# Second attention of a four-layer kernel: a shift chain of four operations with ScalarE's copy and its rows in two lots, and selections dealt out anew over the steps

## The reference

```python
def _L1_attn_ref(x, w_attn, w_proj):
    H, HEAD_D = 16, 8                      # D = 128
    qkv = x @ w_attn
    q = qkv[..., :D].reshape(Bv, Tv, H, HEAD_D).transpose(0, 2, 1, 3)
    k = qkv[..., D:D + HEAD_D]
    v = qkv[..., D + HEAD_D:]
    att = jnp.einsum('bhqd,bkd->bhqk', q, k) * scale
    att = jnp.where(causal[None, None, :, :], att, -jnp.inf)
    att = jax.nn.softmax(att, axis=-1)
    y = jnp.einsum('bhqk,bkd->bhqd', att, v)
    y = y.transpose(0, 2, 1, 3).reshape(Bv, Tv, D)
    return y @ w_proj
```

## Time and profile before

| | us |
|---|---|
| median of 3 runs | 826.43 (826.15 to 827.19) |
| the profiled execution | 826.32 |
| its span, first to last instruction | 824.6 |
| PE busy | 658.2 |
| DVE busy | 567.6 |
| ACT busy | 348.2 |
| POOL busy | 348.9 |

### The profile page before, as it was taken

How to read it: one execution, slowest core, us unless ns; L and a number is a source line. 1 busy time by engine, 2 the same in 40 slices (tenths; PEclk the granted TensorE clock), 3 DMA queues, 4 the chain that set the end, 5 groups by cost and what they waited for, 6 DMA issues and landing times. The chain is left out here.

```text
span 824.6 us, 14720 instructions
## 1 busy us (share of the span) xinstructions
PE 658.2 (80%) x4409; PEld 408.9 (50%) x4409; DVE 567.6 (69%) x1843; ACT 348.2 (42%) x748; POOL 348.9 (42%) x510
## 2 busy tenths in 40 slices
PE   1589898987008999999965779899898989898684
PEld 1346565655005788777842234445454535353353
DVE  8378888886862322444366978798979898884373
ACT  0422223311703222323321047677676767676751
POOL 0165555661027777677511014343434344333320
PEclk9999999999558999999965669999999999999995
DMA  9300000000411222222234304030303031200020
GB/s 295 97 1 1 0 1 0 0 2 1 144 38 49 43 42 36 39 42 40 24 76 62 45 11 59 4 60 10 53 14 51 21 43 26 37 2 4 1 77 27
DMA packets 40353, 32.47 MB, mean 39 GB/s; under 512 B 3608, under 2 KB 36936, under 8 KB 40280
## 3 DMA queue, kind: packets, MB, share of 16 engines
q1 hardware_dynamic: 30448, 23.51, 13.2%
q0 software_dynamic: 7840, 6.86, 5.7%
q10 hardware_dynamic: 1992, 1.21, 0.9%
HBM read 13.60 MB, written 8.13 MB: 26 GB/s over the span
## 5 line engine op out<-in xcount | busy, mean ns | idle before, releaser
L1613 ACT ACTIVATE pexp<-wide 128x512 f32<-128x512 f32 (+2 forms) x384 | 181.5, 535 | 108.8 <-PE wide L1802 107.3
L1544 POOL TENSOR_SCALAR_AFFINE_SELECT pexp<-pexp 128x256 f32<-128x256 f32 x256 | 105.0, 414 | 202.5 <-ACT pexp L1613 200.3
L1419 DVE CUSTOM_DVE_ANT_0 masked<-bank,mask_qk 128x384 f32<-128x384 f32 (+3 forms) x356 | 154.4, 480 | 22.0 <-PE bank L1753 21.1
L1802 PE MATMUL wide<-qT,kTe 128*128 128x256 bf16 (+3 forms) x512 | 121.8, 305 | 10.2 <-ACT pexp L1613 5.2
L1753 PE MATMUL bank<-kTm,qT 128*128 128x384 bf16 (+3 forms) x356 | 90.9, 323 | 16.4 <-DVE mx L1419 10.2
L1070 ACT ACTIVATE hT<-wide,b1T 128x512 f32<-128x512 f32 x64 | 44.0, 687 | 137.2 <-PE wide L1090 137.2
L1419 DVE CUSTOM_DVE_ANT_0 masked<-wide,mask_qk 128x256 f32<-128x256 f32 (+3 forms) x156 | 74.2, 498 | 18.6 <-PE wide L1753 18.6
L938 POOL DMA_INDIRECT x_row<-xln_dram,row_u x64 | 63.4, 991 | 52.8 <-DVE slot_tok L815 33.6
L1815 PE MATMUL bank<-pexp,vx 128*32 128x512 f32 (+3 forms) x1024 | 83.5, 444 | 0.0
L945 POOL DMA_INDIRECT x_dram<-yg,row_u x40 | 63.8, 1595 | 31.3 <-DVE yg L994 21.6
L561 POOL TENSOR_TENSOR kv<-kx,qv 128x1024 f32<-128x1024 f32 x32 | 62.3, 1949 | 24.1 <-PE wide L636 24.1
(11 more groups left out here) (232 smaller groups left out, 1086.7 us busy)
## 6 DMA issues: line engine op xcount, KB each, us to landing
qT<-qp SPq DMA_DIRECT2D x135, 64.0 KB
x_sb<-in_L_attn_x SPq DMA_DIRECT2D x8, 256.0 KB, 6.9
w_sb<-in_L_ffn_w SPq DMA_DIRECT2D x1, 2048.0 KB, 12.8
xln_dram<-rx SPq DMA_DIRECT2D x8, 256.0 KB, 2.3
out_x<-x_sb SPq DMA_DIRECT2D x8, 256.0 KB, 2.3
x_dram<-x_sb SPq DMA_DIRECT2D x5, 256.0 KB, 3.5
x_sb<-x_dram SPq DMA_DIRECT2D x5, 256.0 KB, 2.9
x_row<-xln_dram,row_u POOLq DMA_INDIRECT x64, 2.5
```

Source lines behind the costliest of these rows:

```text
L1419: ins = nc.vector.tensor_tensor_reduce(out=masked[:, n % 4, at], in0=bank_of(n)[:, at], in1=mask_qk[:, T - w:T], scale=1.0, scalar=LEAST, ...
L1544: nc.gpsimd.affine_select(out=pexp[:, at, :, 0:P], in_=pexp[:, at, :, 0:P], pattern=[[0, 2], [1, P]], compare_op=ALU.is_ge, fill=0.0, base ...
L1613: nc.scalar.activation(pexp[:, exp_slot(b, 2 * step + h // 2), h % 2:h % 2 + nh, 0:w], psE[m % 3][:, 0:nh * w].rearrange("p (h t) -> p h t ...
L1802: ins = nc.tensor.matmul(psE[m % 3][:, hh * w:(hh + 1) * w], kTe[:, par, j * P:(j + 1) * P], qT[:, b % QB, 4 * qd + h + hh, j * P:T], star ...
```

## The change

Four things, all in the second attention.

1. `split` has four operations instead of five: the last subtraction writes the third part as bf16 at once, in place of a subtraction and a copy. It serves the shift (VectorE), q (VectorE; the operation at 5 C goes) and k (GpSimd).
2. The copy to `mT` moves from VectorE to ScalarE (`act_shift_T`), at the head of its step 13, behind the exponentials of step 13 and ahead of those of step 14. TensorE's transposes move from 12 D to 13 A, behind the first scores of step 14.
3. The one DMA of the shift's rows becomes six: for quad 0 one for each part (4 heads each), then for the other three quads one for each part (12 heads each). The scores of step 0 wait for the first three, those of step 4 for the last three.
4. `IN_STEP` changes from (4,3,2,2,1,2,2,2,5,4,3,3,2,4,2,3) to (4,4,4,3,1,2,2,2,4,4,3,3,1,2,2,3). `AHEAD`, the selections of steps 12 to 15, falls from 11 to 8, and steps 0 to 3 take 15 instead of 11. The order within each turn and the banks follow from the same rule as before.

```diff
+        SPLITS = 2 * PARTS - 2
...
-        IN_STEP = (4, 3, 2, 2, 1, 2, 2, 2, 5, 4, 3, 3, 2, 4, 2, 3)
+        IN_STEP = (4, 4, 4, 3, 1, 2, 2, 2, 4, 4, 3, 3, 1, 2, 2, 3)
...
             for n in ops:
                 if n:
                     engine.wait_ge(sig.sem, sig.at(b, n))
+                if n == SPLITS - 1:
+                    on.tensor_tensor(parts[-1], rest, parts[-2], ALU.subtract).then_inc(sig.sem, 1)
...
-        def dve_shift_T(dve, b):
-            dve.wait_ge(q_mTp.sem, q_mTp.at(b, 1))
-            dve.wait_ge(q_mrow.sem, q_mrow.at(b, 0))
-            nc.vector.tensor_copy(mT[:, :], psA[:, :].bitcast(BF16)[0:PARTS * HEADS, 0:T]).then_inc(q_mT.sem, 1)
...
+        def act_shift_T(act, b):
+            act.wait_ge(q_mTp.sem, q_mTp.at(b, 1))
+            for rows in q_mrow:
+                act.wait_ge(rows.sem, rows.at(b, 0))
+            nc.scalar.activation(mT[:, :], psA[:, :].bitcast(BF16)[0:PARTS * HEADS, 0:T], ACT.Copy).then_inc(q_mT.sem, 1)
...
             for s in range(STEPS):
+                if middle and s == SHIFT_STEP + 1:
+                    act_shift_T(act, b + 1)
...
             sp.wait_ge(q_mT.sem, q_mT.at(b, 1))
-            sp.dma_start(qT[QR:QR + PARTS, b % QB, :, :], mT[:, :]).then_inc(q_mrow.sem, 16)
+            for rows, lo, hi in ((q_mrow[0], 0, 4), (q_mrow[1], 4, HEADS)):
+                for n in range(PARTS):
+                    sp.dma_start(qT[QR + n:QR + n + 1, b % QB, lo:hi, :],
+                                 mT[n * HEADS + lo:n * HEADS + hi, :]).then_inc(rows.sem, 16)
...
             if step == 0:
-                pe.wait_ge(q_mrow.sem, q_mrow.at(b, 1))
+                pe.wait_ge(q_mrow[0].sem, q_mrow[0].at(b, PARTS))
                 pe.wait_ge(q_kTe.sem, q_kTe.at(b, 1))
+            if step == NT:
+                pe.wait_ge(q_mrow[1].sem, q_mrow[1].at(b, PARTS))
...
+                    if middle and (s, place) == (SHIFT_STEP + 1, "A"):
+                        pe_shift(pe, b + 1, front)
                     if place == "D":
                         if s % 2:
                             pe_values(pe, b, s - 1)
                             pe_values(pe, b, s)
-                        if middle and s == SHIFT_STEP:
-                            pe_shift(pe, b + 1, front)
```

More of the change, by code:

```diff
@@ L1190, in build @@
         Q = lambda name, per=1, step=1: signal("mqa_" + name, per, step)
+        SPLITS = 2 * PARTS - 2
         q_init = Q("buffers_set")
         q_xln, q_xTp, q_xT, q_qp = Q("xln", NT), Q("xT_psum"), Q("xT"), Q("q_psum")
-        q_kvp, q_kv, q_kpart, q_qpart = Q("kv_psum"), Q("kv"), Q("k_parts", 5), Q("q_parts", 5)
+        q_kvp, q_kv, q_kpart, q_qpart = Q("kv_psum"), Q("kv"), Q("k_parts", SPLITS), Q("q_parts", SPLITS)
         q_v, q_kx = Q("v"), Q("k_slots", PARTS)
@@ L1209, in build @@
         PER_QUAD = NM // NQ
-        q_smp, q_mx, q_mpart = Q("max_scores_psum", NM), Q("max", NM), Q("max_parts", 5)
-        q_mTp, q_mT, q_mrow = Q("max_T_psum"), Q("max_T"), Q("shift_rows", 1, 16)
+        q_smp, q_mx, q_mpart = Q("max_scores_psum", NM), Q("max", NM), Q("max_parts", SPLITS)
+        q_mTp, q_mT = Q("max_T_psum"), Q("max_T")
+        q_mrow = [Q(f"shift_rows_{lot}", PARTS, 16) for lot in ("first_quad", "other_quads")]
         NX = NQ * NT * 2
@@ L1255, in build @@
         XLN_STEPS, XT_STEP, Q_STEP, KV_STEP, K_SPLIT_STEP, SLOT_STEP, KT_STEP = (0, 1), 2, 3, 5, 6, 7, 8
-        Q_SPLIT_STEPS = (4, 5)
+        Q_SPLIT = {(4, "A"): 1, (4, "C"): 2, (5, "A"): 3}
         RESIDUAL_STEP = 6
@@ L1362, in fill_k_slots, with split @@
             return ops(kx3[:, :, :, n, :], kp[:, n].unsqueeze(2).broadcast_to([P, NT, PARTS, L]))
-        def split(engine, on, sig, b, whole, rest, parts, ops=range(2 * PARTS - 1)):
+        def split(engine, on, sig, b, whole, rest, parts, ops=range(SPLITS)):
             for n in ops:
-                part = parts[n // 2]
                 if n:
                     engine.wait_ge(sig.sem, sig.at(b, n))
-                if n % 2 == 0:
-                    on.tensor_copy(part, whole if n == 0 else rest).then_inc(sig.sem, 1)
+                if n == SPLITS - 1:
+                    on.tensor_tensor(parts[-1], rest, parts[-2], ALU.subtract).then_inc(sig.sem, 1)
+                elif n % 2 == 0:
+                    on.tensor_copy(parts[n // 2], whole if n == 0 else rest).then_inc(sig.sem, 1)
                 else:
-                    on.tensor_tensor(rest, whole if n == 1 else rest, part, ALU.subtract).then_inc(sig.sem, 1)
+                    on.tensor_tensor(rest, whole if n == 1 else rest, parts[n // 2], ALU.subtract).then_inc(sig.sem, 1)
         def dve_q_parts(dve, b, ops):
@@ L1388, in pool_k_slots @@
         def pool_k_slots(pool, b):
-            pool.wait_ge(q_kpart.sem, q_kpart.at(b, 5))
+            pool.wait_ge(q_kpart.sem, q_kpart.at(b, SPLITS))
             pool.wait_ge(q_kTp.sem, q_kTp.at(b, 0))
@@ L1462, in dve_turn @@
                         dve_shift(dve, b + 1)
-                    if middle and s == SHIFT_STEP + 1 and place == "A":
-                        dve_shift_T(dve, b + 1)
                     if middle and s < SHIFT_STEP:
@@ L1472, in dve_turn @@
                         dve_stats(dve, b - 1)
-                    if front and s in Q_SPLIT_STEPS and place in "AC":
-                        dve_q_parts(dve, b + 2, (2 * Q_SPLIT_STEPS.index(s) + "AC".index(place) + 1,))
+                    if front and (s, place) in Q_SPLIT:
+                        dve_q_parts(dve, b + 2, (Q_SPLIT[s, place],))
         def dve_ln3_shift(dve, lo, hi):
@@ L1495, in mqa_dve @@
             dve_moe_stats(dve, 4)
-            dve_q_parts(dve, 0, range(1, 5))
+            dve_q_parts(dve, 0, range(1, SPLITS))
             nc.vector.memset(mask_qk[:, 0:T - P], 0.0)
@@ L1511, in mqa_dve @@
             dve_max(dve, 0, range(PER_QUAD, 2 * PER_QUAD), bank_at_start)
-            dve_q_parts(dve, 1, range(1, 5))
+            dve_q_parts(dve, 1, range(1, SPLITS))
             dve_max(dve, 0, range(2 * PER_QUAD, NM), bank_at_start)
             dve_shift(dve, 0)
-            dve_shift_T(dve, 0)
             dve_max(dve, 1, range(AHEAD), bank_in_turn)
@@ L1625, in act_yT, with act_turn @@
             nc.scalar.activation(y2T[:, :], psT[:, :], ACT.Copy).then_inc(q_yT.sem, 1)
-        def act_turn(act, b, tail=True, front=True):
+        def act_turn(act, b, tail=True, middle=True, front=True):
             for s in range(STEPS):
+                if middle and s == SHIFT_STEP + 1:
+                    act_shift_T(act, b + 1)
                 if s % NT == 0 and (s or b):
@@ L1676, in mqa_act @@
             act.wait_ge(s_shift.sem, s_shift.total(4))
+            act_shift_T(act, 0)
             act_exp(act, 0, 0)
             for b in range(B):
-                act_turn(act, b, tail=b > 0, front=b + 2 < B)
+                act_turn(act, b, tail=b > 0, middle=b + 1 < B, front=b + 2 < B)
             act_quad(act, B - 1, NQ - 1)
@@ L1690, in q_rows @@
             for n in range(PARTS):
-                queue.wait_ge(q_qpart.sem, q_qpart.at(b, 2 * n + 1))
+                queue.wait_ge(q_qpart.sem, q_qpart.at(b, min(2 * n + 1, SPLITS)))
                 for j in range(PARTS):
@@ L1779, in pe_shift @@
         def pe_shift(pe, b, front):
-            pe.wait_ge(q_mpart.sem, q_mpart.at(b, 5))
+            pe.wait_ge(q_mpart.sem, q_mpart.at(b, SPLITS))
             if front:
```

## The result

The changed kernel takes 823.06 us (median; 819.06 to 825.08) against 826.70 of the kernel before beside it (823.57 to 830.71). The ratio is 0.9952, with a 95% interval of 0.9936 to 0.9969: faster by about 4 us, where the forecast was slower by 5.4. The time lies inside the forecast's range of 820.5 to 838.5, but on the other side of before. The profiled execution of the changed kernel took 824.32 us.

What follows compares the result with a forecast made beforehand. Each turn was taken as a loop from rows' arrival to last selection to next arrival, with no engine full; 826.32 + 3.0 (turns and start) + 2.4 (clock falls) = 831.7 us, range 820.5 to 838.5.

Steps and rivals of the forecast that it cites:

- the loop: A second-attention turn: rows' arrival to last selection, 32.1 us, plus last selection to next arrival, 7.2; only these count.
- The path without the rows: Shift, chain start to first DMA: shorter chain and ScalarE copy make it 1.23 + 0.45 to the copy, then 0.60.
- the 4.2: Shift rows, first DMA issue to PE's start: three DMAs would take 4.2 us where one took 3.66.
- the failed step: Shift rows: 1.3 us from packets to PE's start, seen with one 48-row DMA, was kept for the small DMAs.
- My lower bound, 2.9: Shift rows, issue to PE's start: 2.9 us if each small DMA's issue takes only 0.28.
- The rival of cheap DMAs: Shift rows: issues of 0.3 us each make the path 5.3, a turn 38.6, the kernel 820.2; chance 0.23.
- The selections: Three more selections behind the rows' arrival make the last selection 1.2 us later, bounds 0.6 and 1.6.
- steps 8 and 9 give 0.4 back: Steps 8 and 9 hold one selection of 512 less while DVE is full, recovering 0.4 us.
- The start: Turn 0 of the second attention: first scores at 482.8 instead of 484.67, 1.9 us earlier, bounded by the rows.
- the limit that I had worked out and set aside: Start of turn 0: scores stand behind the selections ahead; 8 instead of 11 lowers this limit by 1.85 us.
- The clock: PE's wait of about 2 us at turn ends drops its clock; 0.8 us per fall, three falls, +2.4 us.
- the rival of a fall in every turn: PE clock falls every turn at full price: 829.3 + 7 x 1.3 = 838.4 us; chance 0.05.

Runs made afterwards that it cites:

- quad_old_deal: Changed kernel with the previous IN_STEP and each quad's shift rows in one DMA of twelve rows: 813.87 us, ratio 0.9836 to the kernel before.
- quad_rows: Changed kernel with mp laid out by quads, parts, heads, one DMA of twelve shift rows per quad: 818.97 us, ratio 0.9909 to the kernel before.
- deal_later: Changed kernel, still 8 selections ahead, but three selections dealt to steps 4, 6 and 7 instead of 1 to 3: turns of 39.15 us, one execution.
- new_deal_only: Kernel before with only the new IN_STEP: 829.87 us, ratio 1.0047 to the kernel before.
- old_deal: Changed kernel with the previous IN_STEP, 11 selections ahead: 814.62 us, ratio 0.9866 to the kernel before.
- one_dma: Changed kernel with all 48 shift rows moved by the one DMA of before: 826.41 us, ratio 1.0003 to the kernel before.
- dve_copy_old_deal: Changed kernel with the mT copy back on VectorE and the previous IN_STEP: turns 1, 2 and 4 took 38.5 us, turns 3 and 5 39.96 and 39.99.
- five_ops: Changed kernel with splits of five operations again for shift, q and k: turn 3 took 39.37 us, one execution.
- dve_copy: Changed kernel with the copy to mT back on VectorE at 13 A, new IN_STEP kept: turn 39.33 us, one execution.

## Why the prediction was wrong, point by point

**What bounds the kernel: right for before and after.** Where the rows end last, each edit moved its own piece of the loop and the turn by as much: the deal 1.57, the fifth operation 0.23, the copy 0.2 or 0.9, the lots 0.6. It isn't the whole rule: where PE's own work reaches as far as the rows (quad_old_deal) 0.8 us taken from the path gained nothing, and with 12 ahead both pieces grew. The path without the rows was forecast as 1.68 + 0.60 and measured as 1.67 + 0.62. That ScalarE delays its exponentials of step 14 harmed nobody, as said: they ran from 635.53, and no wait of PE behind them is for one.

**The rows: here it failed.** Two terms of the 4.2 were mis-sized. The issues took 0.65, 0.61 and 0.57, not 0.70, and the third ended 1.92 after the first began, not 2.18, which is 0.3 in the sum. And the time between the last packet and PE's start was taken over from the large DMA, 1.3 us. This is the failed step: three small DMAs take 3.07 us, less than the one large DMA's 3.66, and not 4.2. The DMA view of after, in slices of 0.1 us from 635.6, shows three small groups of packets, best seen in its second line, and then a fourth, larger one, which belongs to the other quads:

```profile
DMA  0000000000000000000000000010000000320000
GB/s 0 0 0 0 0 0 0 0 0 0 0 0 0 21 21 0 0 0 0 0 31 10 0 0 0 0 31 10 0 0 0 0 0 0 72 52 0 0 0 0
```

The third group moves at 638.2 to 638.3, and PE starts at 638.72, 0.35 later. In the earlier trace rows packets stop at 638.9 and PE starts at 640.2. So what I had added as a fixed cost grows with the transfer. The packet and landing records of the traces, over all turns, say the same for three sizes. From a DMA's last write (four bytes, behind an engine's rows) to its last landing it is 0.31 to 0.34 us for four rows, one on each of four engines (after); 0.57 to 0.64 for twelve rows, four on each of three engines (quad_rows); 1.26 to 1.37 for 48 rows, sixteen on each of three engines (before). Whether rows behind one another on an engine make the tail, or rows in all, these three don't separate, since both grow. The first DMA of the other quads in after, twelve rows on twelve engines, took 0.54 to 0.55 in six of its eight times, nearly as much as the twelve rows on three, so the number on an engine isn't the whole of it, and the cause stays open. With 0.35 in place of 1.3 the forecast's sum would have been 3.2 against 3.07 measured. My lower bound, 2.9, varied the issue alone and kept the 1.3, so it was reached by the wrong road. That the measured time lies inside the range is luck. The rival of cheap DMAs, at 0.23, had the right sign by the wrong mechanism: the issues were not cheap.

In that place I weighed a rule of the Trainium skill (DMA: Bandwidth & Descriptors, "Why a DMA increments its semaphore by 16 and not by 1") by the order of issue times. After has 0.57 to 0.66 for four rows on four engines and 0.72 to 0.76 for twelve rows on twelve, the other way round than fewer engines and more increments by SP would have it. The traces do agree with the rule on the increments: for four rows the semaphore has five updates, one ahead of all packets and four behind them, and for the one DMA of before, which ran on three engines, one and three. By the rule that one DMA has SP write thirteen and a small one twelve, so it never spoke against the small ones singly, only against there being three. It doesn't order the issue times here, and the measurement decides.

**The selections: right in kind, somewhat too small.** 1.57 instead of 1.2, inside the bounds and at their upper end. That steps 8 and 9 give 0.4 back, and that DVE's gaps take a part, was not so: deal_later, which leaves step 8 at five, paid the same 1.57. The sign itself was there: from 602.3 to 613.1 DVE has a single wait, of 0.15.

**The start: right in size, wrong in reason.** 2.3 instead of 1.9. The rows were not what bounded it: in after they were issued at 480.06 and the scores came at 483.76, 3.7 later where a landing takes 3.07, and quad_rows, whose rows land 0.8 sooner, needs the same 58.62 from the first ACTIVATE to the first exponential. What bounded it was the limit that I had worked out and set aside, the selections ahead. new_deal_only, with three fewer of them, gains 1.56 (59.34 against 60.90), and old_deal, with the rest of the change, 0.72 (60.18); together 2.28. Of the 0.72, 0.44 stand before the first selection, where GpSimd's split of k is one copy shorter, and 0.23 in the shorter chain. The copy of q on VectorE gave nothing: the first selection and the first shift are earlier by the same 0.44.

**The clock: the mechanism exists, and didn't act in the turns.** PE's wait for the rows was 0.66 and not about 2 us, and neither it nor one_dma's 1.25 in each turn was followed by a fall in turns 1 to 5, so 2.4 us of the forecast were not there. The price was too low as well: 0.8 for a fall, where dve_copy_old_deal shows 1.5. The 1.3 in the rival of a fall in every turn has no working, and no run shows it. At the end of turn 6 the row's wait of 1.62 holds the missing record of the first scores, so it was 1.38 against 1.61 before, and no fall came; PE was busy for at least 1.79 us of the stretch around it, where before it was 1.47. What decides between a fall and none isn't shown. The windows answer to the earlier trace rows:

```profile
754.32 0.59 PE L1811 MATMUL wide<-qT,kTe 128*128 128x512 bf16 x2 [1.62 <-DMA qT<-mT]
```

```profile
750.96:754.37 3.41, 1.79 (x21) 1.00 0.03 7
754.37:757.79 3.42, 2.95 (x27) 1.00 0.04 10
```

A fall that before has there and after hasn't would be most of the 1.2 us that after gained from turn 7 on, where nothing was changed. Over all kernels here that part, from turn 7's first exponential to the last operation, took between 63.8 and 67.0 us, and the two ends belong to kernels with the same work there, so I count it as chance and not as the change's work. Without it the profiled gain is 2.6 us, nearly all of it at the start.

**The sum again.** 3.7 us = 2.3 at the start, 0.4 in turn 0, 0.5 in turns 1 to 5, -0.6 in turn 6, 1.2 from turn 7 on (3.8, rounded). The forecast had +0.5 for turn 0 and +1.4 for turn 6. In one of turns 1 to 5 (turn 2) after was 0.4 slower than in the others, as one_dma, quad_rows and five_ops were by 0.4 to 0.5; the cause stays open. With the arrival at its true 3.07 the forecast's own steps would have given 829.3 - 7 x 1.1 = 821.6 without falls of the clock, on the right side of before. The profiled 824.32 is 2.7 more, of which 1.3 stand ahead of the second attention and 1.9 are five turns of selections at 1.57 instead of 1.2.

## What to carry to other kernels

When a small transfer ends a loop, take its cost apart into issue, first packet, packets and landing, and measure each on a transfer of its own size: the tail behind a large transfer is no fixed price. Work that is dealt out over a loop should stand where the loop waits anyway (here ahead of the rows' arrival), and its count there mattered more than its balance elsewhere; once the wait was covered, more of it ahead cost time on both sides of the arrival. Before a wait is used as a number, look whether the record of the instruction that ended it is missing: here that made 0.89 out of 0.66. A change of four parts can be faster as a whole and hold a part that loses nearly all of the gain: undo each part alone.

## What the runs showed of the hardware

- The last landing of a DMA from SBUF to SBUF came 0.31 to 0.34 us after its last write for four rows of 1 KB on four engines (after), 0.57 to 0.64 for twelve on three (quad_rows), 0.54 to 0.55 for twelve on twelve (after), 1.26 to 1.37 for 48 on three (before).
- Its issue on SP took 0.57 to 0.66 us for four rows (after), 0.70 to 0.79 for twelve (after, quad_rows), 0.73 to 0.80 for forty-eight (before, one_dma): it hardly follows the amount of data.
- ScalarE's copy of 48x512 bf16 out of PSUM took 0.59 us (after), VectorE's 0.41 (before, dve_copy).
- One fall of the PE clock to 0.50 within a turn cost 1.5 us (dve_copy_old_deal), and it came in two of five turns with the same waits.
